# Layer 2's residual sum made by TensorE and put back by ScalarE, and the forward step-size sums half a slot on

## What is computed

```
x  = layernorm(gn(v)) @ W_in_x.T ;  z = layernorm(gn(v)) @ W_in_z.T      # 192 -> 384 channels
# forward over x, and backward over x reversed, each with its own weights:
xc = silu(causal_conv4(x))
dbl = xc @ W_xproj.T                          # 12 columns for dt, 16 for B, 16 for C
dt = softplus(dbl[:, :12] @ W_dt.T + dt_bias)
h  = h * exp(dt * A) + (dt * xc) * B          # 16 states a channel
y  = sum_n(h * C) + xc * D
# then
out = (y_forward + y_backward) * silu(z) @ W_out.T + b_out
v  = v + out                                  # the sum that the change moves
```

## Time and profile before

| | us |
|---|---|
| median of 3 runs | 20129.69 |
| lowest and highest | 20121.38, 20151.25 |
| the profiled execution | 20123.45 |
| its span, first to last instruction | 20121.7 |

### The profile page before, as it was taken

How to read it: one execution, slowest core, us unless ns; L and a number is a source line. 1 busy time by engine, 2 the same in 40 slices (tenths; PEclk the granted TensorE clock), 3 DMA queues, 4 the chain that set the end, 5 groups by cost and what they waited for, 6 DMA issues and landing times. The chain is left out here.

```text
span 20121.7 us, 179901 instructions
## 1 busy us (share of the span) xinstructions
PE 17468.9 (87%) x43392; PEld 7664.0 (38%) x43392; DVE 17219.6 (86%) x13583; ACT 13992.6 (70%) x35077; POOL 16825.7 (84%) x10932
## 2 busy tenths in 40 slices
PE   7888988889888898888988889888898888988889
PEld 3433434334343343433434334343343433434334
DVE  7988979889798897988979789797897978979789
ACT  6767767577676776767767577675776767767677
POOL 6978969789697896978969799696996979969699
PEclk9989989899899998989989899898998989989899
DMA  2313323133231332313323133231332313323233
GB/s 85 135 65 129 137 76 134 65 129 137 76 134 66 128 137 76 134 65 128 137 77 133 66 128 136 77 133 65 129 136 76 134 65 135 130 77 135 73 132 124
DMA packets 528855, 2178.88 MB, mean 108 GB/s; under 512 B 96328, under 2 KB 243424, under 8 KB 527648
## 3 DMA queue, kind: packets, MB, share of 16 engines
q1 hardware_dynamic: 527648, 2165.99, 29.8%
HBM read 1905.47 MB, written 245.63 MB: 107 GB/s over the span
## 5 line engine op out<-in xcount | busy, mean ns | idle before, releaser
L1032 DVE TENSOR_TENSOR_SCAN arena<-ps,arena 128x897 f32<-128x897 f32 x5376 | 10963.7, 2066 | 993.9 <-ACT arena L1188 761.6
L1240 POOL TENSOR_TENSOR arena<-arena 128x896 f32<-128x896 f32 x5376 | 9427.4, 1769 | 901.5 <-PE ps L962 619.8
L962 PE MATMUL ps<-arena,ident 128*128 128x448 f32 x21504 | 8979.4, 556 | 879.6 <-POOL arena L1240 876.2
L1172 ACT ACTIVATE ps<-arena,A 128x448 f32<-128x448 f32 x10752 | 6412.1, 632 | 1749.0 <-DVE arena L1032 1705.3
L962 PEld LDWEIGHTS ps<-arena,ident 128*128 128x128 f32 x21504 | 4049.3, 193 | 5473.3 <-issue 3690.3
L1232 POOL TENSOR_TENSOR arena<-arena 128x896 f32<-128x896 f32 x2688 | 4773.6, 1776 | 0.2 <-DMA arena<-bc_rows 0.2
L1021 DVE TENSOR_TENSOR arena<-ps,arena 128x896 f32<-128x896 f32 x2688 | 2868.0, 1067 | 30.4 <-ACT ps L1134 30.4
L919 PE MATMUL ps<-arena,diag 128*128 128x448 f32 x5376 | 2178.4, 549 | 154.0 <-issue 141.8
L919 PEld LDWEIGHTS ps<-arena,diag 128*128 128x128 f32 x5376 | 1014.8, 192 | 1233.9 <-issue 1097.4
L1094 ACT ACTIVATE arena<-ps,vece 128x448 f32<-128x448 f32 x672 | 423.3, 630 | 948.5 <-PE ps L919 948.5
L1188 ACT ACTIVATE arena<-arena 128x2 f32<-128x2 f32 x5376 | 1045.8, 195 | 50.9 <-DVE arena L1032 50.9
(11 more groups left out here) (160 smaller groups left out, 19406.9 us busy)
## 6 DMA issues: line engine op xcount, KB each, us to landing
arena<-bc_rows SPq DMA_DIRECT2D x1792, 896.0 KB, 5.4
x_projected<-arena SPq DMA_DIRECT2D x112, 672.0 KB, 3.5
y_forward<-arena SPq DMA_DIRECT2D x112, 672.0 KB, 3.9
arena<-x_projected SPq DMA_DIRECT2D x112, 672.0 KB, 7.7
arena<-y_forward SPq DMA_DIRECT2D x112, 672.0 KB, 4.1
x<-in_x SPq DMA_DIRECT2D x119, 336.0 KB, 3.6
x_normed<-arena SPq DMA_DIRECT2D x112, 336.0 KB, 2.8
arena<-x_normed SPq DMA_DIRECT2D x112, 336.0 KB, 4.2
```

Of the source, the lines that this page charges most:

```text
L962: m = e.matmul(y, ident[:, :], pr[:, q % NPR, a * T:a * T + T], start=False, stop=p == NP - 1 and a == 1)
L1032: e.tensor_tensor_scan(rev(hh[:, q % NH, 0:W2], s), rev(decays(q)[:, 0:W2], s), rev(bb[:, q % NB, 0:W2], s), car[:, k, n:n + 1] if i % NC ...
L1172: e.activation(two(decays(q))[:, a, :], dt[:, r % NDT, :], ACT.Exp, scale=Am[s][:, k, 2 * p + a:2 * p + a + 1]).then_inc(c_ex, 1)
L1240: e.tensor_tensor(pr[:, q % NPR, :].rearrange("p (a b) -> p a b", a=2), two(hh[:, q % NH, :]), cr[:, 2 * p:2 * p + 2, :], ALU.mult).then_i ...
```

## The change

In layer 2 the output projection gets a fourth matmul: the identity times `x1`'s piece, into the same bank. The bank then holds projection and residual, and `ou` only has to add the bias and write `x1`. That is now an Identity activation on ScalarE, due 2.4 slots behind the projection and not 1.5. The store is due 0.9 slots later, but keeps its place in SyncE's list. The forward chunks' `td` are due at t + 3.4 and not t + 2.9, and all `du` at t + 4.2 and not t + 3.9.

```diff
--- before.py
+++ after.py
@@ -74,8 +74,8 @@
     def step_size(i, e, t):
         pe.append((t, "t", i, e))
         act.extend([(t + 1, "t1", i, e), (t + 2, "t2", i, e), (t + 2.6, "t3", i, e)])
-        dve.append((t + 2.9, "td", i, e))
-        pool.append((t + 3.9, "du", i, e))
+        dve.append((t + (2.9 if CHUNK[i][0] else 3.4), "td", i, e))
+        pool.append((t + 4.2, "du", i, e))
         act.append((max(NP * (EJ * i + e) - 2, t + 4.5), "dp", i, e))
 
     def project(i, t, u, v):
@@ -120,8 +120,8 @@
             for k in range(CJ):
                 o = t + 2 * PER + (4, 6)[k]
                 pe.append((o, "o", i, k))
-                dve.append((o + 1.5, "ou", i, k))
-            sp.append((o + 2.5, "out", i, 0))
+                act.append((o + 2.4, "ou", i, k))
+            sp.append((o + 3.4, "out", i, 0))
             sp.append((t + PER + 4, "yl", i, 0))
         for e in range(EJ):
             t = NP * (EJ * i + e + 1) + LAG - 1
@@ -940,9 +940,8 @@
                     o = job(name, i, k)
                     for j in range(EJ):
                         w.wait_ge(c_yv, EJ * (i - NC) + j + 1)
-                        m = e.matmul(o[0:CP, :], wout[:, j, k * CP:(k + 1) * CP], gy[:, j, :],
-                                     start=j == 0, stop=j == EJ - 1)
-                    m.then_inc(c_wt, 1)
+                        e.matmul(o[0:CP, :], wout[:, j, k * CP:(k + 1) * CP], gy[:, j, :], start=j == 0, stop=False)
+                    e.matmul(o[0:CP, :], ident[0:CP, 0:CP], x1[:, k, ch(c)], start=False, stop=True).then_inc(c_wt, 1)
 
         side(-10)
         for g in range(-2, Q + LAG):
@@ -1006,12 +1005,6 @@
                     if i > NC:
                         filled(w, "o", i - 1, CJ - 1)
                     e.tensor_tensor(gy[:, k, :], gz[:, k, :], ps[:, YBANK, 0:T], ALU.mult).then_inc(c_yv, 1)
-                if name == "ou":
-                    filled(w, "o", i, k)
-                    b = bank_of("o", i, k)
-                    x = x1[:, k, ch(c)]
-                    e.scalar_tensor_tensor(x, ps[0:CP, b, 0:T], bout[:, k:k + 1], x, ALU.add,
-                                           ALU.add).then_inc(c_wf[b], 1)
 
         def product(q):
             r, i, k, p, s = pair(q)
@@ -1136,6 +1129,11 @@
                     w.wait_ge(c_sm, NP * (r + 1))
                     w.wait_ge(s_yw, 16 * i)
                     e.activation(gy[:, k, :], ps[:, YBANK, 0:T], ACT.Copy).then_inc(c_ya, 1)
+                if name == "ou":
+                    filled(w, "o", i, k)
+                    b = bank_of("o", i, k)
+                    e.activation(x1[:, k, ch(c)], ps[0:CP, b, 0:T], ACT.Identity,
+                                 bias=bout[:, k:k + 1]).then_inc(c_wf[b], 1)
                 if name == "z1":
                     filled(w, "z", i, k)
                     o = ps[:, bank_of("z", i, k), 0:T]
```

## The result

| | before | after |
|---|---|---|
| median, us | 20140.47 (4 runs) | 20293.56 (4 runs) |
| lowest and highest | 20121.38, 20151.98 | 20287.02, 20310.45 |
| the profiled execution | 20123.45 | 20296.23 |

The ratio of the times is 1.0078 with a 95% interval of 1.0061 to 1.0096. The kernel is slower, as forecast, but by twice as much: 153 us by the medians, where the prediction had 74 above the profiled execution, 70 above the median. 20293.56 lies just above the range.

The account below looks back on a forecast made before the run. It took TensorE's run in layer 2's backward chunks with projections as the bound, GpSimd being late afterwards; 120 + 24 - 40 - 30 = +74 us gave 20200 us, forecast range 20170 to 20250, wider range 20110 to 20290.

Parts of the forecast that it names:

- What bounds the kernel: Layer 2's backward chunks: while the projections run, TensorE is late and the others wait; afterwards GpSimd is late.
- Part 1: Added projection matmuls, 0.75 us each on TensorE: 120 us in five chunks plus 24 us at the end, +144 us.
- Part 2: Residual sum leaves VectorE, freeing 195.2 us with waits; costed at zero, at most 208 us gained.
- Rival A: Backward chunks with projections: VectorE is the end, so freeing it shrinks them, 208 us, to about 19880; chance 0.08.
- the rule that stood beside it from the Trainium skill: Relieve the engine with highest occupancy; read TensorE's headroom from weight loads, 38% busy, so TensorE would have room.
- Part 3: Write-back on ScalarE behind the projections: waits hidden by idle time, zero; +96 us if that cover failed.
- Part 4, forward: Later step-size sums and products close a 0.42 us GpSimd wait in six forward chunks: 40 us off.
- The late bank: Forward chunks: third step-size matmul starts about 1.9 us later, hidden by TensorE's 2.62 us idle; uncovered, +182 us.
- Part 4, backward: Backward half: second L1221 product moves behind one product, same GpSimd work ahead of the critical product, so zero.
- Part 5: Backward chunks: TensorE dips to 1.2 GHz, 0.98 us each; longer chunks lose step with them, 30 us off (0 to 78).

Follow-up runs that it names:

- e1: The kernel after with the backward chunks' du due at t + 3.9 again, forward ones still at t + 4.2: 20158.64 us, ratio 1.0015.
- e2: The kernel after with td at t + 2.9 and du at t + 3.9 everywhere: 20177.31 us, ratio 1.0025.
- e4: The kernel after without the added matmul, which leaves out the residual sum: 20144.86 us, ratio 1.0009.
- e6: The kernel after with the added identity matmul made twice: 20428.66 us, ratio 1.0156.
- e8: e5 with the third block's convolution in backward chunks due at t + 11.2, not t + 10.7: 20026.89 us, ratio 0.9956.
- e7: The kernel before with only the write-back moved to ScalarE, no matmul added, residual sum left out: 20123.47 us, ratio 1.0003.
- e5: The kernel before with td at t + 3.4 and du at t + 4.2 in forward chunks only: 20104.42 us, ratio 0.9998.
- e3: The kernel before with only the step-size changes, td and du timed as in the kernel after: 20155.14 us, ratio 1.0013.
- e10: e8 with the second block's convolution in backward chunks due at t + 9.2, not t + 8.7: 19977.91 us, ratio 0.9915.
- e9: e8 with the residual sum on TensorE and the write-back on ScalarE: 20156.48 us, ratio 1.0007.

## Why the prediction came out half as large

**What bounds the kernel: right.** The chain after is the one described. Work taken from or added to the TensorE run moves a chunk with the same stretches by the work's own length (e1, e2, e4, e6), and a change of order alone in that run moved the time (e8).

**Part 1, the matmuls, +144 us: right.** Chunks without a stretch grew by 1.46 to 1.49 us (1.50), the end by 1.51 us, and e6 against e4 gives 0.75 us a matmul. Over the whole time e4 gives 139 to 149 us and e6 135 to 157, with shifts of the clock in both that nearly cancel. The last chunk was taken as covered; it grew by 0.4 us.

**Part 2, VectorE's freed time at zero: right** (e7, 1.0003). Rival A falls with it. So does, for this kernel, the rule that stood beside it from the Trainium skill (Perfetto Trace Analysis, Identifying the Most-Contended Engine): TensorE's weight loads read 39% after, and yet its in-order queue was what the others waited for.

**Part 3, ScalarE at zero: right** (e7, which shows parts 2 and 3 together). Its waits are 0.57 us and 0.96 us, under 1 as forecast:

```profile
20154.45 0.63 ACT L1135 ACTIVATE x<-ps,bout 96x448 f32<-96x448 f32 x1 [0.57 <-PE ps L944]
...
20160.47 0.63 ACT L1135 ACTIVATE x<-ps,bout 96x448 f32<-96x448 f32 x1 [0.96 <-PE ps L944]
```

**Part 4, forward: the mechanism right, the size too large.** The same place in three forward chunks after, for the earlier trace rows, is 70.39 us apart, where it was 70.84:

```profile
19422.81 3.27 PE ps L905 x8
...
19493.20 3.27 PE ps L905 x8
...
19563.59 3.27 PE ps L905 x8
```

The late bank showed as a wait of 1.99 us and cost nothing in these chunks, as said (about 1.9 us, hidden):

```profile
19400.56 1.01 PE L931 MATMUL ps<-arena,wdt 12*128 12x448 f32 x2 [1.99 <-DVE arena L1000]
```

But chunk 5, the last of the six, grew from 70.71 to 72.36 us, 26 us over the images. So of 40 us only 7 were left in the forward half of the kernel after, and e1 has 19 over e2. Two things add up in chunk 5. Without a stretch it is 71.4 us with the forward changes (all sixteen in e5, three in after), 0.7 above before. With one that begins 7 us into it, it is 72.6 us, and thirteen images of the kernel after have that. The later bank alone doesn't bring these: e5 has the same forward changes and none, e1 seven. What brings them, and the 0.7 us, stays open.

**Part 4, backward: the step that failed.** It read: "In the backward half only the second L1221 moves behind one product; the same GpSimd work stands ahead of the product at 19969.04, so zero." The GpSimd work ahead of that product is indeed the same. But zero was the price for GpSimd alone, with nothing for what TensorE does in the meantime. The product between no longer has the second L1221 in front of it: it comes earlier, TensorE does its sum earlier, and then idles longer ahead of the run (1.68 us before and in e1, 2.1 to 2.5 in after and e3). The low clock then falls on the head of the run. The moved step costs 127 to 135 us beside the residual matmuls (e1 against after), and some 30 to 50 us without them (e3 against e5, hardly more than their intervals tell apart), where the prediction had zero. That it is the step is shown by these runs; that it acts through the idle time is what the traces show side by side, as no run lengthened the idle time in another way:

```profile
20137.60 1.77 PE L961 MATMUL ps<-arena,ident 128*128 128x448 f32 x4 [2.08 <-POOL arena L1238]
```

This is one of thirteen backward chunks of the kernel after in which TensorE idled 2.08 or 2.09 us; none of them has an early stretch. Of the 67 in which it idled 2.12 to 2.5 us, 65 have one.

**Part 5, the clock, -30 us: the sign was wrong; this step failed with the one above.** I saw that a chunk of another length would lose the rhythm of the dips, and took it that dips could only go. In e2 they did: 22 late ones for 61. Its backward chunks grew by 80 us where the matmuls make 117, so some 37 us came back there. As much came back between the images, and so the matmuls alone cost only 44 to 54 us. In the kernel after, the late ones rose to 75 and early ones came, at a place where each costs some 2 us. Counted over the 80 chunks, 225 us were added, of which the matmuls make 118; 107 are the clock's. On the other side the time from one image's last scan to the next one's first fell from 265.5 to 262.75 us, though the projections in it grew by 1.5 us. That is some 65 us, most of it in layer 1, whose code the change doesn't touch. The traces point at the clock here too: of each such time TensorE spent 107 us at the low level before and 96 us after, and among the fifteen of the kernel before, which lie between 262.6 and 271.3 us, the longer ones are those with more time at the low level (correlation 0.84; 0.83 in after). No run sets this clock, so why it shifted stays open.

Added up: 144 for the matmuls, 7 off in the forward half, 107 for the clock in the backward chunks, 65 off between the images, 18 off at the turn, and some 10 in small parts make 171, beside 172.7 measured.

## What to carry to other kernels

Find the engine whose in-order run the others wait for, and price work added to it at its full length, whatever the busy shares say; before taking work off, look whether another order of the same queue gives the awaited result sooner (e8 gained 0.4% with one convolution half a slot later, e10 0.85% with two). A move that leaves the critical product where it was need not be free for TensorE: if it makes TensorE's idle time ahead of its run longer, ask where the low clock will then fall. And where a loop's length and the clock's dips keep step, measure chunks with and without a dip apart, since the mean mixes the two.

## What the runs showed of the hardware

TensorE idling 1.68 us ahead of its run was never followed by the low level at that place in before, e1, e2, e5, e7 or e8 (480 chunks); in 15 of 160 chunks of e9 and e10 a stretch began 9 to 10 us into the chunk all the same. Idling 2.12 to 2.5 us was followed by it in 65 of 67 chunks of the kernel after, idling 2.08 or 2.09 us in none of 13; in e3, with 2.41 us or more, it was in 75 of 80. An early stretch lasted 3.4 us in after and in e3 and slowed the pace to half: the row of the first four sums, 1.77 us without it, took 2.0 to 3.4 us in after and 2.7 to 3.4 us in e3, by how much of it the stretch covered.
